# Exponentials of two score banks at a time in the long slots of an attention pipeline, and the order of TensorE's work that goes with it

## The reference, cut to what matters

```
def _attn(q, k, v, mask):
    scores = jnp.einsum('bqhd,bkhd->bhqk', q, k) / np.float32(np.sqrt(HD))
    scores = jnp.where(mask[:, None, None, :], jnp.float32(-jnp.inf), scores)
    w = jax.nn.softmax(scores, axis=-1)
    return jnp.einsum('bhqk,bkhd->bqhd', w, v)
for i in range(NL):
    ...
    x = x + attention of x with itself, q and k rotated
    x = x + attention of x with the context, q and k rotated
    h = jax.nn.gelu(xn @ f1_w[i].T + f1_b[i], approximate=False)
    x = x + (h @ f2_w[i].T + f2_b[i])
```

## Time and profile before

| What | Value |
|---|---|
| median of three runs | 4006.18 us |
| the profiled execution's own time | 4017.16 us |
| its span, first to last instruction | 4015.4 us |
| TensorE (PE) busy | 3740.2 us, 93% |
| VectorE (DVE) busy | 2789.9 us, 69% |
| ScalarE (ACT) busy | 2486.5 us, 62% |
| GpSimd (POOL) busy | 1099.6 us, 27% |
| mean granted TensorE clock | 0.979 of full speed |

### The profile page before, as it was taken

One profiled execution on the slowest core, in us unless ns is written; L12 is line 12 of the kernel. 1 busy time (PEld: TensorE's weight loads), 2 busy tenths in 40 slices (PEclk: granted clock), 3 DMA queues, 4 the chain that ended last, 5 costly groups with the idle time before them and its releaser, 6 DMA issues. The chain is left out here.

```text
span 4015.4 us, 53044 instructions
## 1 busy us (share of the span) xinstructions
PE 3740.2 (93%) x19504; PEld 1691.6 (42%) x19504; DVE 2789.9 (69%) x4497; ACT 2486.5 (62%) x4213; POOL 1099.6 (27%) x998
## 2 busy tenths in 40 slices
PE   3899999999999999999999999999999999998568
PEld 1233355433355433355433355433355433344457
DVE  5888766688766688766688766688766688752222
ACT  1577665677666677665677665677665677655123
POOL 1332322232322232322232322232322232311324
PEclk8999999999999999999999999999999999999789
DMA  7566443366443366443366443366443366431245
GB/s 184 124 150 147 114 91 81 81 150 149 113 89 83 78 151 145 115 91 82 78 151 144 117 90 83 79 151 147 114 91 96 85 158 161 110 74 43 62 116 100
DMA packets 282259, 448.74 MB, mean 112 GB/s; under 512 B 50824, under 2 KB 190224, under 8 KB 281488
## 3 DMA queue, kind: packets, MB, share of 16 engines
q1 hardware_dynamic: 237328, 378.51, 39.4%
q0 software_dynamic: 44672, 66.83, 7.4%
HBM read 278.54 MB, written 170.15 MB: 112 GB/s over the span
## 5 line engine op out<-in xcount | busy, mean ns | idle before, releaser
L1161 ACT ACTIVATE prob<-ps 128x512 f32<-128x512 f32 x3072 | 1745.5, 596 | 1079.4 <-PE ps L1086 1072.9
L1342 DVE TENSOR_REDUCE negmax<-ps 128x2 f32<-128x1024 f32 x1536 | 1814.6, 1219 | 208.4 <-PE ps L1113 200.4
L1099 PE MATMUL psv<-prob,v 128*32 128x512 f32 x6144 | 820.3, 606 | 0.0
L1086 PE MATMUL ps<-qstack,kstack 114*128 114x512 bf16 x1536 | 564.0, 386 | 24.3 <-ACT prob L1161 19.0
L1086 PE MATMUL ps<-xin,zrow 114*128 114x512 bf16 x1536 | 564.8, 387 | 19.3 <-ACT prob L1161 13.9
L1061 PE MATMUL side<-nT,wf 128*128 128x256 f32 x1536 | 378.8, 390 | 14.8 <-DVE hT L1442 10.5
L1086 PEld LDWEIGHTS ps<-qstack,kstack 114*128 114x128 bf16 x1536 | 142.4, 96 | 575.6 <-ACT prob L1161 372.2
L1086 PEld LDWEIGHTS ps<-xin,zrow 114*128 114x128 bf16 x1536 | 142.1, 96 | 575.0 <-ACT prob L1161 362.0
L865 POOL TENSOR_TENSOR low<-rot,parts 128x1024 bf16<-128x1024 f32 x94 | 200.3, 2130 | 604.1 <-ACT parts L1194 604.1
L1442 DVE TENSOR_SCALAR hT<-side,f1b 128x256 f32<-128x256 f32 x384 | 167.7, 479 | 275.2 <-PE side L1061 266.4
L1072 PE MATMUL side<-wf,hT 128*128 128x256 f32 x1536 | 348.0, 379 | 2.9 <-DVE x L1451 1.6
(11 more groups left out here) (227 smaller groups left out, 3882.2 us busy)
## 6 DMA issues: line engine op xcount, KB each, us to landing
bounce<-parts SPq DMA_DIRECT2D x288, 256.0 KB, 2.5
value_sums<-osum SPq DMA_DIRECT2D x192, 256.0 KB, 6.9
xin<-bounce SPq DMA_DIRECT2D x192, 192.0 KB, 5.7
zrow<-bounce SPq DMA_DIRECT2D x192, 192.0 KB, 6.3
qstack<-bounce SPq DMA_DIRECT2D x192, 192.0 KB, 5.8
kstack<-bounce SPq DMA_DIRECT2D x192, 192.0 KB, 6.4
bounce<-low SPq DMA_DIRECT2D x96, 256.0 KB, 2.1
hT<-value_sums POOLq DMA_DIRECT2D x96, 256.0 KB, 5.2
```

What stands on the lines that cost most here:

```text
L1086: nc.tensor.matmul(ps2[:, n % RING2, :], kk[0:ROWS, h, kt * P:(kt + 1) * P], q[0:ROWS, h, :], start=True, stop=True).then_inc(s_p2full, 1)
L1099: mm = nc.tensor.matmul(psv[32 * i:32 * i + 32, 0, :], v[j % 2][:, kt, (HD + 1) * h:(HD + 1) * h + 32], prob[:, 4 * (u % 2) + i, :], start ...
L1161: nc.scalar.activation(prob[:, 4 * (u % 2) + i, :], ps2[:, n % RING2, :], ACT.Exp, scale=HD ** -0.5).then_inc(s_prob, 1)
L1342: nc.vector.tensor_reduce(out_at, ps1[:, 2 * (n % 2):2 * (n % 2) + 2, :], AX, ALU.max, negate=True).then_inc(s_p1free, 1)
```

## The change

It touches the long slots up to slot 48, and there two things.

- ScalarE: the two exponentials of a place become one instruction over both banks of `ps2` (`exp_of_two`). It waits for the second product of the two, and counts `s_prob` up by two at its end. The wait of product n for `s_prob` is left as it was.
- TensorE: a unit's order becomes: two pairs of the first pass, products 0 and 1, the side work of the even place, the value products, products 2 and 3, the side work of the odd place.

```diff
+        def is_by_two(k):
+            return is_ffn(k) and k <= JOBS
...
+            def by_two(k, p1):
+
+                plan = slot_chunks(k)
+                for u in range(SLOT_UNITS):
+                    if p1:
+                        pass1(k, 2 * u)
+                        pass1(k, 2 * u + 1)
+                    pass2(k - 1, u, 0)
+                    pass2(k - 1, u, 1)
+                    for chunk in plan[2 * u]:
+                        side_work(k, *chunk)
+                    if u:
+                        pv(k - 1, u - 1)
+                    else:
+                        pv(k - 2, SLOT_UNITS - 1)
+                    pass2(k - 1, u, 2)
+                    pass2(k - 1, u, 3)
+                    for chunk in plan[2 * u + 1]:
+                        side_work(k, *chunk)
+
             def slot(k, p2, p1, tail, head):
+                if is_by_two(k):
+                    by_two(k, p1)
+                    return
...
+            def exp_of_two(j, u, i):
+
+                n = 4 * u + i
+                act.wait_ge(s_p2full, 64 * j + n + 2)
+                if i == 0 and (j > 0 or u >= 2):
+                    act.wait_ge(s_pv, 16 * j + u - 1)
+                at = 4 * (u % 2) + i
+                nc.scalar.activation(prob[:, at:at + 2, :], ps2[:, :, :], ACT.Exp, scale=HD ** -0.5).then_inc(s_prob, 2)
...
-                    if p2:
+                    if p2 and is_by_two(k):
+                        exp_of_two(k - 1, u, 2 * half)
+                    elif p2:
                         exp(k - 1, u, 2 * half)
                         exp(k - 1, u, 2 * half + 1)
```

## The result

The changed kernel takes 4118.31 us (median of 4 runs, 4115.41 to 4120.81) against 4006.86 for the kernel before (4 runs, 3999.98 to 4008.03): 1.0282 times as long, 95% interval 1.0264 to 1.0299. The forecast was slower, 4077, with a range up to 4106. The direction and the new waits came out as forecast; the loss is 111 us, not 71, and lies outside the range.

What follows compares the result with a forecast made beforehand. TensorE was taken as the bound. New waits, later reads and fewer array changes summed to 3.06 us per ordinary long slot, 64.3 over 21; with 3.1 and 3.7 more, +71 on 4006 gave 4077 us, range 4046 to 4106.

Steps and rivals of the forecast that it cites:

- The bound: TensorE, busy 93%, sets the time; its new waits lengthen slots one for one, ScalarE's savings are worth nothing unless awaited.
- The long exponential: ScalarE's one exponential over both banks takes 1.04 us, range 0.94 to 1.19, replacing two of 596 ns.
- R: Time from a pair's second product start to the next product that waits for its exponential: 0.43 + 1.04 + 0.05 = 1.52 us.
- the empty places: Places without a side chunk: new TensorE waits of 0.67 us at 5, 15, 31 and 0.20 at 10, 16.
- ScalarE's later reads: Reads of `side` queue 0.44 us later behind the long exponential: LT +0.43, HQ +0.20, GELU -0.22 a slot.
- M: After chunk M the value products follow directly, one change of the array's division less at two places: -0.18 us a slot.
- Changes of the array's division: On TensorE, each change between full and divided array costs some 0.09 us, also behind a side chunk; four a unit before and after.
- The rival with the cheaper change: Changing the array's division is cheaper behind a side chunk, 2.0 us a slot less: 4031 us; chance 0.08.
- Slots 47 and 48: Waits before place 11 vanish into the wait for O; O's late chain and later waits add +3.7 us together.
- TensorE sits idle there, so +0.43: At LT, place 17, the second transposes wait for a ScalarE read that comes later, lengthening the slot by 0.43 us.
- Saves nothing: Rival: the long exponential takes 1.19 us or reading two banks costs more, about 1.3 us a slot: 4107 us; chance 0.08.
- Nothing to measure: Rival: new waits are given back at later ones (LT, HQ, GELU), so the time stays at 4006 us; chance 0.03.

Runs made afterwards that it cites:

- experiment 1: The changed kernel with two single exponentials a place again, TensorE's new order kept: 4019.19 us, ratio 1.0032.
- experiment 7: The changed kernel with the long exponential only at the 17 places with a side chunk of 1.7 us or more, single ones elsewhere: 4023.35 us, ratio 1.0038.
- experiment 6: The changed kernel with ScalarE's copy of the value sums at place 17 behind its first LT read in long slots: 4080.23 us, ratio 1.0182.
- experiment 5: The kernel before, with ScalarE doing the first LT chunk's read twice in long slots up to 47: 4042.87 us, ratio 1.0084.
- experiment 8: The kernel before with the value-sums copy behind the first LT read and, in unit 12, value products ahead of the third product: 3976.98 us, ratio 0.9919.
- experiment 4: The kernel before with the long slots' table moved so the two LT chunks stand at places 17 and 18: 4017.13 us, ratio 1.0029.
- experiment 3: The changed kernel with the long slots' table moved so the two LT chunks stand at places 17 and 18: 4113.35 us, ratio 1.0267.
- experiment 2: The changed kernel with TensorE's old order in all slots, long exponentials kept: 4418.61 us, ratio 1.1040.

## Why the prediction was right in its waits and wrong in its size

**The bound: right.** ScalarE's saving of 77 us bought nothing; what TensorE newly waits for lengthened the slot one for one. Experiments 1 and 7 show it from both sides. The Trainium skill ("Perfetto Trace Analysis", Optimizing Scalar/DVE Operations) says that where ScalarE isn't saturated but makes bubbles on other engines, breaking instructions up may be better. This case agrees: ScalarE was busy 62% before, and joining its instructions made the kernel 1.0282 times as long.

**The long exponential: right.** 1.022 us, taken at 1.04. The estimate of 1.04 by the Trainium skill ("ScalarE: Activation LUTs", What ACT_TABLE_LOAD costs) holds within 0.02 too.

**R and the empty places: right, a little short.** At place 15 the second product starts at 1808.71 + 0.60 - 0.38 = 1808.93, the next pair at 1810.58: 1.65, taken at 1.52. At place 5 the wait is 0.70, so R is 1.55 there. Places 15 and 31 have 0.79. What sets these two apart in the program is that the products behind them, the first of units 8 and 0, also wait for the semaphores of their inputs (`s_second`, `s_mload`); that this makes the 0.09 was not tried. The three odd places cost 2.28 instead of 2.01. Places 1, 3 and 7 cost 0.61 (0.15, 0.27, 0.19) instead of 0.69, places 10 and 16 0.48 instead of 0.40, less the 0.27 as forecast.

**ScalarE's later reads: right in length.** LT +0.48 (0.43 forecast), HQ +0.21 (0.20), GELU -0.19 (-0.22). With M (-0.18), and the chunks of HV at places 1 and 4, which take some 0.1 more each, that makes the 3.6 us of a slot without a fall of the clock, where 3.06 was forecast: 12 us over the 21 slots.

**Changes of the array's division: right.** A product or a side chunk ahead of value products or first pass both have 0.31 from start to start. The rival with the cheaper change is out.

**Slots 47 and 48: right in sum, by luck.** 3.3 us, forecast 3.7. Slot 47 takes 3.5 us more (93.61) and slot 48 0.2 less (92.16), where 1.8 and 1.9 more were forecast. So the sum is right by luck; their clocks, 0.96 and 0.94 instead of 0.98 and 0.93, have a part in it.

**The step that failed: "TensorE sits idle there, so +0.43".** The term at LT had the right wait, and put at nothing what a longer one brings with it. TensorE's idle time there went from 1.41 to 1.89 us, and in 17 of 21 slots instead of one the clock fell behind it. That is 23 us of the 41 by which the forecast was short. Experiment 6 shows that it is this wait: with 0.49 us less of it no slot falls. Experiment 5 shows that neither the new order nor the long exponential is needed. It could have been read from the trace: slot 15 of the kernel before has the same wait with a fall behind it, and takes 92.29 us. The prediction reads slots 23 and 48 alone, and its range had no case for a fall. The waits' 12 us come next; the other 5 or 6 us stay open.

**Rivals.** None of the four was it. "Saves nothing" had the nearest number, 4107, with a wrong cause. "Nothing to measure" fell with the result, and in experiments 6 and 8 a wait that was taken out was gained in full. In experiment 4 it was not: a wait for VectorE that LT's had covered came out, and the one behind the GELU grew.

## What to carry to other kernels

An instruction over two banks reports both free only at its end: with a ring of two, the next product waits for latency plus the whole instruction, here 1.55 us. What it may cost is the list of places where the producer has less other work than that, and the reads that now queue behind it. Work out that list before saving time on an engine that isn't the bound, and use the long form only where the list is covered.

When a wait on TensorE grows, look up in the trace whether the clock fell behind that wait in any repetition, even one in twenty: a half microsecond more can make it the rule, and half a microsecond less can be worth three times itself.

## What the runs showed of the hardware that had not been expected

The granted clock falls to 1.2 GHz, for 3.4 us each time, behind the slot's longest wait of TensorE. In most of these kernels that is the wait between the LT chunks; with LT apart it is the one behind the GELU. Counted over the 21 slots of one profiled execution each, with the idle time before the row:

| Kernel | Wait | Idle time | Slots with a fall |
|---|---|---|---|
| experiment 8 | LT | 0.92 us | 0 |
| experiment 7 | LT | 1.27 | 2 |
| experiment 6 | LT | 1.40 | 0 |
| before | LT | 1.41 | 1 |
| experiment 1 | LT | 1.49 | 3 |
| experiment 4 | GELU | 1.62 | 7 |
| changed kernel | LT | 1.89 | 17 |
| experiment 3 | GELU | 1.98 | 12 |
| experiment 5 | LT | 2.22 | 11 |

In experiment 2, where many waits follow each other, every long slot has one or more. So the number rises steeply with the wait, but is not ordered by its length alone. Slots with the same waits fall and don't fall in one execution (experiment 5, slots 30 and 31; experiment 3, slots 22 and 24), so the moment has a part in it. What TensorE did just ahead may have one too: in the changed kernel waits of 0.79 and 0.24 us at places 15 and 16 stand there, in the kernel before one of 0.27 at place 16 alone. How the two share was not tried.
